# GpSimd's work in another order: products by twos, folds behind them, value rows stored as they are multiplied

## The reference: what is computed

```python
x = x + attn(layernorm(x), Wq, Wk, Wv, Wo)
x = x + xattn(layernorm(x), ctx, Wq, bq, Wkv, bkv, Wp, bp)
x = x + moe(layernorm(x), gate, expert_bias, w1, w2, w3, shared_w1, shared_w2, shared_w3)
```

```python
q, k, v = (x @ Wq.T), (x @ Wk.T), (x @ Wv.T)       # each reshaped to (token, 16 heads, 16)
q, k = rope(q), rope(k)
q = q.reshape(B, S, G, H // G, Dh).transpose(0, 1, 3, 2, 4).reshape(B, S, H, Dh)
scores = einsum('bshd,bstd->bsht', q, k) / sqrt(16)
attn = einsum('bsht,bstd->bshd', softmax(scores), v).reshape(B, S, 256) @ Wo.T
```

## Time and profile before

| | |
|---|---|
| median of 3 runs | 1142.42 us (1141.93 to 1144.45) |
| the profiled execution | 1142.42 us, span 1140.6 us |
| VectorE busy | 947.2 us, 83% of the span |
| TensorE busy | 772.9 us, 68%; mean granted clock 0.862 |
| ScalarE busy | 758.7 us, 67% |
| GpSimd busy | 752.4 us, 66% |
| main loop | from about 114 us, 16 passes |

### The profile page before, as it was taken

How to read it: one execution, slowest core, us unless ns; L and a number is a source line. 1 busy time by engine, 2 the same in 40 slices (tenths; PEclk the granted TensorE clock), 3 DMA queues, 4 the chain that set the end, 5 groups by cost and what they waited for, 6 DMA issues and landing times. The chain is left out here.

```text
span 1140.6 us, 21740 instructions
## 1 busy us (share of the span) xinstructions
PE 772.9 (68%) x7110; PEld 460.5 (40%) x7232; DVE 947.2 (83%) x1939; ACT 758.7 (67%) x987; POOL 752.4 (66%) x792
## 2 busy tenths in 40 slices
PE   6765555767676767677676768676776758667664
PEld 3433222434343444444443435343443435334333
DVE  5895878979797979889797979798898979798952
ACT  2434546587777767685877767676858686768762
POOL 6536887777776777867777767678777777741011
PEclk9877778979798979879798988898888989898986
DMA  6011567979695968689796969787887869697970
GB/s 216 1 38 42 104 120 120 166 123 164 99 167 112 166 121 151 123 140 165 130 158 112 167 102 164 118 158 126 151 146 130 166 113 162 106 171 140 186 135 5
DMA packets 541029, 147.84 MB, mean 130 GB/s; under 512 B 534130, under 2 KB 538868, under 8 KB 540532
## 3 DMA queue, kind: packets, MB, share of 16 engines
q1 hardware_dynamic: 540916, 146.44, 72.1%
HBM read 10.09 MB, written 2.10 MB: 11 GB/s over the span
## 5 line engine op out<-in xcount | busy, mean ns | idle before, releaser
L1033 DVE TENSOR_SCALAR_CACHE_REDUCE score<-ps_score,q_neg 128x1024 f32<-128x1024 f32 x512 | 638.0, 1278 | 38.2 <-PE ps_score L1382 37.3
L734 ACT ACTIVATE prob<-score,exp_bias 128x2048 uint16<-128x2048 f32 x256 | 511.4, 1999 | 96.1 <-DVE exp_bias L1043 95.7
L1382 PE MATMUL ps_score<-keys,queries 128*128 128x512 bf16 x902 | 311.8, 424 | 150.2 <-DVE score L1033 127.2
L521 POOL TENSOR_TENSOR product<-hs_exp,v_tok 128x1024 f32<-128x1024 f32 x64 | 183.6, 2869 | 56.2 <-ACT hs_exp L702 56.2
L527 POOL TENSOR_TENSOR folded<-product 128x512 f32<-128x512 f32 x128 | 163.3, 1275 | 40.8 <-POOL product L521 30.5
L1400 PE MATMUL ps_pv<-prob_t,values 128*32 128x128 f16 x4096 | 158.8, 239 | 45.1 <-DMA prob_t<-prob 45.0
L1400 PEld LDWEIGHTS ps_pv<-prob_t,values 128*32 128x32 f16 x4096 | 135.0, 106 | 109.8 <-issue 109.8
L1382 PEld LDWEIGHTS ps_score<-keys,queries 128*128 128x128 bf16 x1024 | 71.4, 104 | 256.9 <-DVE score L1033 221.8
L521 POOL TENSOR_TENSOR product<-qk_rot 128x1024 f32<-128x1024 f32 x64 | 150.4, 2351 | 0.6 <-POOL qk_rot L507 0.5
L763 ACT ACTIVATE routed_both<-normed,routed_gate 128x256 bf16<-128x256 f32 x124 | 52.7, 496 | 98.1 <-POOL routed_gate L490 98.1
L962 DVE TENSOR_REDUCE hs<-folded 128x64 f32<-128x256 f32 x64 | 26.5, 416 | 69.8 <-POOL folded L532 69.7
(11 more groups left out here) (129 smaller groups left out, 1130.2 us busy)
## 6 DMA issues: line engine op xcount, KB each, us to landing
prob_t<-prob SPq DMA_TRANSPOSE x256, 4.5
prob_t<-in_w SPq DMA_DIRECT2D x3, 1024.0 KB, 4.8
x_in<-in_x SPq DMA_DIRECT2D x16, 128.0 KB, 2.8
score<-in_cond_t SPq DMA_DIRECT2D x4, 512.0 KB, 6.9
out<-x_out SPq DMA_DIRECT2D x16, 128.0 KB, 2.6
w_qkv<-in_w_qkv SPq DMA_DIRECT2D x1, 768.0 KB, 4.3
early<-in_w_kv SPq DMA_DIRECT2D x1, 512.0 KB
w_s<-in_w_s SPq DMA_DIRECT2D x3, 128.0 KB
```

The costliest lines, as they stand in the source:

```text
L521: pool.tensor_tensor(product[:, r], a_, b_, ALU.mult).then_inc(multiplied, 1)
L734: act.activation(prob[:, s, :].bitcast(U16), score[:, s, :], ACT.Exp, bias=exp_bias[:, s:s + 1], scale=-1.0, accum_out=prob_sum[:, t.par, ...
L1033: dve.tensor_scalar(score[:, s, HALF * i:HALF * i + HALF], ps_score[:, i].rearrange("p b k -> p (b k)"), q_neg[:, t.par, h:h + 1], None, A ...
L1382: mm = pe.matmul(ps_score[:, i, b, :], queries[:, t.par, h // 2, h % 2, :], keys[:, h // 2, k0:k0 + KEYS], start=True, stop=True)
```

## The change

`fold` is taken apart into `multiply`, `fold` and `fold_more`, and steps go by twos: two products, then their two folds, then (for scores) their two second folds. With this the order in a pass of GpSimd is written anew. `ln_scale(2, m)` stands behind the first two score products, `ln_scale(1, n)` between the two second folds, `choose(m)` behind the products 2 and 3 and ahead of their folds. In pass 0 `norm_ho(n)` stands behind the first two score products. `FOLDED` holds what `fold_done` counts to at the fold of step i in the new order. On VectorE `reduce_scores` moves from heads 9, 10, 12 and 13 to 10, 11, 14 and 14, `largest_score` from 13 to 14, and `reduce_values` 0 to 3 from the ends of heads 0 to 3 to heads 1, 2, 3 and 4; on ScalarE `head_exp(a)` moves from ahead of the exponential of head 13 to behind it. `v_tok` becomes `[P, HD, H]`; ScalarE writes it turned. No instruction is added or removed.

```diff
+FOLDED = (1, 2, 5, 6, 9, 10, 11, 12)
...
-        v_tok = sb("v_tok", [P, H, HD])
+        v_tok = sb("v_tok", [P, HD, H])
...
+            def multiply(i, t, a_, b_):
+                if (due := t.due(12, FOLDED[i - 2] - (12 if i < 2 else 0))) is not None:
                     pool.wait_ge(fold_done, due)
                     pool.sem_inc(settled, 1)
-                pool.tensor_tensor(product[:, r], a_, b_, ALU.mult).then_inc(multiplied, 1)
+                pool.tensor_tensor(product[:, i % 2], a_, b_, ALU.mult).then_inc(multiplied, 1)
+
+            def fold(i, t):
+                r = i % 2
                 pool.wait_ge(multiplied, t.count(8, i + 1))
                 pool.sem_inc(settled, 1)
...
+            def fold_more(i, t):
+                r = i % 2
+                pool.wait_ge(fold_done, t.count(12, FOLDED[i]))
+                pool.sem_inc(settled, 1)
+                pool.tensor_tensor(folded[:, r, :, :, 0:HD // 4], folded[:, r, :, :, 0:HD // 4],
+                                   folded[:, r, :, :, HD // 4:HD // 2], ALU.add).then_inc(fold_done, 1)
...
-                v = v_tok[:].rearrange("p t d -> p d t")
-                fold(G + j, t, pr.unsqueeze(2).to_broadcast([P, G, HD, H]),
-                     v.unsqueeze(1).to_broadcast([P, G, HD, H]))
+                multiply(G + j, t, pr.unsqueeze(2).to_broadcast([P, G, HD, H]),
+                         v_tok[:].unsqueeze(1).to_broadcast([P, G, HD, H]))
...
+                if m.exists():
+                    spread_sums(m)
+                if a.exists():
+                    rope(a)
+                    score_products(0, a)
+                    score_products(1, a)
+                if n.exists() and t.starts():
+                    norm_ho(n)
+                if m.exists():
+                    ln_scale(2, m)
...
+            def all_scores(t):
+                for j in range(0, G, 2):
+                    score_products(j, t)
+                    score_products(j + 1, t)
+                    for i in (j, j + 1):
+                        fold(i, t)
+                    for i in (j, j + 1):
+                        fold_more(i, t)
...
-                    act.copy(v_tok[:].rearrange("p h d -> p (h d)"), bank[7][:, 0:D]).then_inc(qkv_kept, 1)
+                    act.copy(v_tok[:].rearrange("p d h -> p h d"), heads(bank[7][:, 0:D])).then_inc(qkv_kept, 1)
...
+                    if a.exists() and h == 14:
+                        head_exp(a)
                     if m.exists() and h in (13, 14):
                         keep_routed(h - 13, m)
-                    if a.exists() and h == 13:
-                        head_exp(a)
...
-                        if h in (9, 10, 12, 13):
-                            reduce_scores((9, 10, 12, 13).index(h), a)
+                        if h in (10, 11):
+                            reduce_scores(h - 10, a)
+                        if h == 14:
+                            reduce_scores(2, a)
+                            reduce_scores(3, a)
...
                         if h in (1, 2) and not t.starts():
-                            reduce_values(h, n)
+                            reduce_values(h - 1, n)
+                        if h == 4 and not t.starts():
+                            reduce_values(3, n)
...
-                        if h in (0, 3):
-                            reduce_values(h, n)
+                        if h == 3:
+                            reduce_values(2, n)
...
-                        if h == 13:
+                        if h == 14:
                             largest_score(a)
```

99 lines of the change are left out of this document (51 added, 48 removed).

## The result

The kernel after takes 1104.39 us (median of four runs, 1097.95 to 1105.85), where the kernel before took 1143.43 on the same chip. The ratio is 0.965, 95% interval 0.961 to 0.969. The forecast of 1100 with a range of 1086 to 1120 held. The profiled execution of the kernel after is its fastest, 1097.95 us with a span of 1096.2, so the spans differ by 44.4 us where the medians differ by 39.0. Working with rows, I split the 44.4, and keep in mind that every row of the kernel after comes from an execution 6.4 us under its median.

The account below looks back on a forecast made before the run. The prediction took a ring of GpSimd, ScalarE and VectorE legs, 62.2 us a tile, to bound the kernel. 13 tiles x 2.6 = 34, plus 8 in tile 0, is 42: 1142.4 - 42 = 1100 us, range 1086 to 1120.

Parts of the forecast that it names:

- The ring: GpSimd, ScalarE and VectorE legs that close a tile: from 62.2 to 59.6 us, 2.6 less; chance 0.55.
- Leg 1: GpSimd from `norm_ho` to the end of `choose`: from 31.0 to 26.5 us, 4.5 less.
- Leg 2: ScalarE from the start of `route` to the end of `hidden_tanh`: stays 16.1 us, `head_exp` with 3.2 of slack.
- rival D: `head_exp` on ScalarE delayed behind the last two score reductions, kernel slower, 1180 us; chance 0.04.
- Leg 3: VectorE from the expert product to the next `norm_ho`: 15.05 + 2.4 - 0.7 + 0.15 = 16.9 us.
- VectorE's slack: VectorE keeps 5 us of waits a tile, where 8 were: before `shared_tanh`, head 15 and the expert product.
- rival C: VectorE held by GpSimd's memory accesses, as `gate_scores` beside the third score product; 1122 us, mild form near 1112; chance 0.24.
- C's sign: Small VectorE instructions take over 1 us in tiles 1 to 13 if GpSimd's memory accesses hold them.
- The layout: Value rows stored turned: GpSimd's value product from 2.87 to 2.35 us, worth 0 to 7 us in all.
- the Trainium skill's ratio for stepped reads: GpSimd reads with a step over 8 bytes cost about 50% an element; value product would fall to 1.9 us.
- ScalarE's stepped write: ScalarE writes `v_tok` with a step: from no change to 0.35 us more, hidden beside ScalarE's waits.
- The ends: Tile 0 gains 8 us (4 to 10); the prologue before 110 us and the end after 1049 us gain 0.

Follow-up runs that it names:

- e3: Kernel after plus one more GpSimd product of 1.89 us a tile, right ahead of `choose`: 1126.03 us.
- e4: Kernel after plus the same extra GpSimd product of 1.89 us a tile, but right behind `choose`, its folds and the bias: 1106.29 us.
- e7: Kernel after with only `choose` moved, behind the third and fourth score sets' folds and second folds: 1148.62 us.
- e5: Kernel after with VectorE's `reduce_values(3)` moved from behind head 4 to behind head 3: 1081.77 us.
- e11: Kernel after plus one VectorE instruction of 1.21 us a tile behind head 13's bias, which nobody waits for: 1103.81 us.
- e6: Kernel after with `choose` one product earlier, between the third and fourth score products: 1101.07 us.
- e8: Kernel after with both edits, `reduce_values(3)` behind head 3 and `choose` ahead of the fourth score product: 1076.53 us.
- e12: e8 plus one VectorE instruction of 1.21 us a tile behind head 13's bias, which nobody waits for: 1104.38 us.
- e1: Kernel after with the value rows `v_tok` stored as before, the new order kept: 1113.09 us.
- e9: Kernel after with VectorE's 8-element addition for the expert scores split into 7 elements and 1: 1104.17 us.

## Why the prediction was right, point by point

- **The ring.** Right in mechanism, and the size nearly so: 59.6 us was forecast and 59.48 measured; since the tile of before was taken as 62.2 and is 62.50 in the mean, the gain is 3.0 a tile and not 2.6. That the tile agrees to 0.1 us is in part luck: it is the tile of the fastest of four executions, and one at the median has, as an estimate, 0.5 us more. e3, e4, e7 and e5 each lengthen or shorten one leg, and the tile follows; e4 and e11 add work off the ring, and it doesn't.
- **Leg 1.** 26.5 forecast, 26.45 measured. The term that counted is the fold, second fold and waits that left the path ahead of `choose`; e7 puts four instructions (two folds, two second folds) back ahead of it and loses all.
- **Leg 2.** 16.1 forecast, 16.07 measured. `hs_exp` had 3.1 us in hand where 3.2 were worked out, so rival D's wait never came (it came in e6 and e8, 0.26 us, and in e12, 1.39). ScalarE waits 81.4 / 16 = 5.1 us for `routed_gate`; 4 to 5 were forecast.
- **Leg 3.** 16.9 forecast, 16.76 measured. In the mean over the twelve tiles its terms hold: the waits for value folds that went are 0.77 us (0.7 forecast), and VectorE's waits for TensorE's scores grew from 0.51 to 0.64, by 0.13 (0.15 forecast). It was read from one tile, and there luck helped: that tile has two fold waits, 0.68 and 0.42, of which only the first was counted, and no wait for scores. In the tile shown of the kernel after, leg 3 is 17.72, with 1.48 of such waits.
- **VectorE's slack.** Here a step failed, without cost. Idle times of 2.2, 1.5 and 1.2 us were forecast before `shared_tanh`, head 15 and the expert product. Measured: 0, 1.58 and 0 in the tile shown, where the expert product starts 0.05 us behind ScalarE's end; at head 15 it goes from 0 to 3.23 over the twelve tiles, 1.07 in the mean. The missing waits went to the held instructions, 2.3 us in that tile, which is rival C's mechanism at the place that it named (`gate_scores` beside the third product). C's sign, small instructions over 1 us in tiles 1 to 13, came true; its price of 1 us a tile didn't. The slack just covered the holds: in eleven of the twelve tiles the expert product starts within 0.05 us of ScalarE's end. That this was near the edge shows in e6, where VectorE has 1.3 us more of work a tile (21.2 / 16) and nearly the whole gain is gone.
- **The layout.** The product came down to 2357 ns as forecast (2.35). Its worth was put at 0 to 7 us; on top of the order it measured 8.7, which the intervals of the two kernels (0.961 to 0.969 and 0.972 to 0.975) can't tell from 7, and in the kernel before 17.6, which is clearly more. The fold waits that it removes on top of the order were sized well (0.35 us a tile, 0.55 at most forecast); what e1 has beside them are longer waits for TensorE's scores, which the prediction's sum for the layout did not have. By the Trainium skill's ratio for stepped reads (GPSIMD Engine Reference, Performance pitfalls for Q7 kernels) the product would have fallen to 1.9 us, an estimate; this did not come.
- **ScalarE's stepped write.** A cost of 0 to 0.35 us was bounded; it is 0.22, and hidden. Line 725 of the kernel after, beside the earlier trace rows:

```profile
L725 ACT COPY v_tok<-ps x16: 572/574/601, 14.3 to 912.8; 128x256 f32<-128x256 f32 x16
```

- **The ends.** For the first pass 8 (4 to 10) were forecast and 6.9 came by pass 1's `norm_ho`. The four waits of the earlier trace rows are gone; in the same stretch VectorE's waits for TensorE's scores grew from 5.5 to 10.2 us. `norm_ho` stands at 148.96 where 149.5 was forecast. The end was taken as 0 and gives back 1.1.
- **The 4.4 us to the median.** The sum was 42 against one profiled execution; the two profiled ones differ by 44.4 and the medians by 39.0. What makes the kernel after spread over 1098 to 1106 stays open, as only its fastest execution has rows. Those of e9 point at TensorE's clock: e9 has the same median, its rows come from an execution of 1107.02 us, and there VectorE's waits for scores are 55.3 us in all instead of 41.6, leg 3 is 17.42 with 1.28 of such waits, and legs 1 and 2 are the same.

## What to carry to other kernels

Before moving work on an engine that is neither the busiest nor idle, close the ring: write one step of each engine that releases the next, from an instruction to the same one a tile later, and change only what lies on it; the same 1.9 us a tile cost 22 us in all right ahead of the choice and nothing that could be measured behind it. Then ask what the busiest engine has left once the ring is shorter, because gains of two legs stop adding there (e5, e6 and e8). And look for small VectorE instructions on on-chip tiles beside GpSimd's long ones: what they take is not their own size but what is left of the instruction they stand beside, and it costs time once the engine has no wait left to cover it. Last, read a leg from many tiles and not from one: leg 3 varied by 1.75 us from tile to tile.

## What the runs showed of the hardware that I had not expected

- An addition on 8 elements took 1.35 us in the mean over 16 tiles beside a product, 0.16 while GpSimd waited (e8). That is 19 us more of VectorE's time in the kernel after.
- Splitting it into 7 and 1 changes nothing (1.33), and a two-input form on 16 elements is held too (0.85).
- ScalarE's copy of 128x256 out of PSUM took 0.58 us with a step of 64 bytes on the writing side and 0.35 without.
- GpSimd's product with one operand stepped by 64 bytes took 2.87 us, 2.36 with both in order: 22%.
- GpSimd pays as well: two folds took 2.81 us where `q_parts` had started 0.09 us ahead of them, 2.48 with nothing of the kind beside them.
- TensorE's 32 products of two heads with the values took 1.07 us at a granted clock of 1.00 and 1.89 at 0.50, and of the twelve tiles the two without a wait for scores in leg 3 are the ones at 1.00 there.
